# Two rearrangements in a four-layer transformer kernel: the first token half's output part moved into the last attention turn, the second half's beside the last layer; block transposes of the first attention done four groups at a time

## The reference, cut to what matters

```python
x = x + _layernorm(_L0_attn_ref(_layernorm(x)))  # delta-rule attention in chunks of 32 tokens
x = x + _layernorm(_L0_ffn_ref(_layernorm(x)))   # 4-head attention and a mixture of 8 experts
x = x + _layernorm(_L1_attn_ref(_layernorm(x)))  # 16-head attention, then the output part below
x = x + _layernorm(_L1_ffn_ref(_layernorm(x)))   # the last layer: w1, w2, h1, h2, w3
```

```python
A = where(strict_lower, -einsum('bhnck,bhnjk->bhncj', k_beta, k), 0)
for i in range(1, 32): A[..., i, :] += einsum('bhnj,bhnjc->bhnc', A[..., i, :], A)
T = A + eye(32)
local_short, local_long = fir(v, firs), fir(v, firl)
```

```python
out = res + _lin(out, Wf, bf)                                  # wf
return out + _lin(relu(_lin(_ln(out, g2, b2), Wr1, br1)), Wr2, br2)   # hid, ffn
h = silu(tlin(x, w1)) * tlin(x, w2)                            # w1, w2
h = gelu(tlin(gelu(tlin(h, h1)), h2)); return tlin(h, w3)      # h1, h2, w3
```

## Time and profile before

| | us |
|---|---|
| median of 3 runs | 965.95 |
| lowest, highest | 960.08, 970.67 |
| the profiled execution | 958.38 |
| its span, first to last instruction | 956.6 |
| PE, DVE, ACT, POOL busy | 701.7, 583.4, 441.9, 85.3 |
| mean granted clock of TensorE | 0.815 |

### The profile page before, as it was taken

How to read it: one execution, slowest core, us unless ns; L and a number is a source line. 1 busy time by engine, 2 the same in 40 slices (tenths; PEclk the granted TensorE clock), 3 DMA queues, 4 the chain that set the end, 5 groups by cost and what they waited for, 6 DMA issues and landing times. The chain is left out here.

```text
span 956.6 us, 14446 instructions
## 1 busy us (share of the span) xinstructions
PE 701.7 (73%) x5339; PEld 574.5 (60%) x5339; DVE 583.4 (61%) x1332; ACT 441.9 (46%) x907; POOL 85.3 (9%) x98
## 2 busy tenths in 40 slices
PE   3993886998863379550896066999999955659996
PEld 2442786998433248450785043888888844438775
DVE  4118999986286346431332955599998765664474
ACT  3332624543452555320353554555555523467584
POOL 0003202200000100106143002000000001000000
PEclk9997757778885579855698557999999986879998
DMA  5200090000600100002111023111111000000000
GB/s 165 45 0 0 2 152 2 1 1 4 256 1 0 67 1 2 0 3 77 37 32 58 12 88 125 46 45 46 47 55 35 1 1 0 1 1 0 1 23 23
DMA packets 36675, 34.85 MB, mean 36 GB/s; under 512 B 18448, under 2 KB 34704, under 8 KB 35840
## 3 DMA queue, kind: packets, MB, share of 16 engines
q1 hardware_dynamic: 35360, 31.38, 11.1%
q0 software_dynamic: 1248, 2.57, 0.8%
HBM read 20.32 MB, written 5.23 MB: 27 GB/s over the span
## 5 line engine op out<-in xcount | busy, mean ns | idle before, releaser
L2271 PE MATMUL PS<-VXF,PT 128*128 128x128 f32 x1024 | 129.8, 280 | 2.1 <-ACT PT L2293 2.1
L2271 PEld LDWEIGHTS PS<-VXF,PT 128*128 128x128 f32 x1024 | 119.5, 192 | 9.6 <-ACT PT L2293 2.9
L2379 DVE TENSOR_REDUCE MX<-PS 128x2 f32<-128x512 f32 x128 | 81.8, 687 | 30.5 <-PE PS L2236 30.3
L2293 ACT ACTIVATE PT<-PS 128x512 f32<-128x512 f32 x128 | 68.6, 596 | 19.5 <-PE PS L2241 19.4
L2308 ACT ACTIVATE UB<-PS 128x292 f32<-128x292 f32 x64 | 26.5, 415 | 60.2 <-PE PS L2271 60.2
L404 PE MATMUL PS<-XT,WT 128*128 x96 | 42.3, 595 | 1.0 <-ACT XT L290 1.0
L2233 PE MATMUL PS<-SPLIT 32*128 32x256 f32 x256 | 39.3, 325 | 3.1 <-DVE MX L2379 3.1
L1908 ACT ACTIVATE HT<-PS,PB 128x128 f32<-128x128 f32 x92 | 26.3, 368 | 24.4 <-PE PS L1866 18.7
L2606 ACT ACTIVATE PB<-PS,PB 128x512 f32<-128x512 f32 x48 | 33.0, 698 | 7.7 <-PE PS L2521 7.7
L2723 DVE TENSOR_TENSOR HBL<-PB,HBH 128x512 fp32r<-128x512 f32 x32 | 22.1, 690 | 22.6 <-ACT PB L2606 17.5
L2236 PE MATMUL PS<-SPLIT 32*128 32x256 f32 x256 | 32.4, 334 | 3.6 <-DVE MX L2379 2.4
(11 more groups left out here) (471 smaller groups left out, 1759.2 us busy)
## 6 DMA issues: line engine op xcount, KB each, us to landing
SPLIT<-SPLIT SPq DMA_DIRECT2D x64, 128.0 KB, 2.1
PB<-in_pb SPq DMA_DIRECT2D x1, 5016.0 KB, 17.9
PB<-in_pd SPq DMA_DIRECT2D x1, 2888.0 KB, 10.1
X<-in_x SPq DMA_DIRECT2D x2, 1024.0 KB, 4.8
X<-fir_rows SPq DMA_DIRECT2D x2, 1024.0 KB, 6.6
TR<-fir_rows SPq DMA_DIRECT2D x2, 1024.0 KB, 8.6
PA<-in_pa SPq DMA_DIRECT2D x1, 1731.0 KB, 8.5
PC<-in_pc SPq DMA_DIRECT2D x1, 1560.0 KB, 6.4
```

The costliest lines, as they stand in the source:

```text
L2271: last = nc.tensor.matmul(PS[:, UM.bank(n), col:col + P], PT[:, k % 4, c, f * P:(f + 1) * P], v, start=(c == 0), stop=(c == 1))
L2293: nc.scalar.activation(PT[:, k % 4, :, :], PS[:, UM.bank(n), :].rearrange("p (c q) -> p c q", c=2), ACT.Exp).then_inc(c_act, 1)
L2379: nc.vector.tensor_reduce(MX[:, :, k], PS[:, UP_.bank(n), :].rearrange("p (f q) -> p f q", f=2), AX.X, ALU.max, negate=True).then_inc(p_dv ...
```

## The change

First attention. (1) The windows and fir 0 and 1 come first on PE, and DVE empties fir 0 and 1. (2) The short filter stands ahead of invert(0). (3) ACT gathers the four diagonal blocks into `BLOCKS`, DVE transposes all 128 partitions by one instruction, the same at the end of the inversion, and ACT spreads the result into `TBD`, for x = 0 after fir 6, for x = 1 after `"ws"` of half 0.

```diff
+            for w in range(2):
+                events += [(("win", w, j), "A", next_bank()) for j in range(4)]
+            events += [(("fir", e), "V", [8 - EARLY + e]) for e in range(EARLY)]
...
-                        pe.wait_ge(a2_tbd, 4 * x + 4)
+                        pe.wait_ge(a2_spread, 4 * x + 4)
...
+                            if (q, h) == (1, NH - 1):
+                                F.wait_taken(act, key)
+                                if x:
+                                    act.wait_ge(a2_in, x)
+                                for c in range(4):
+                                    own = slice(SUB * c, SUB * c + SUB)
+                                    copy(BLOCKS[own, :, :], GR[x][own, :, own]).then_inc(a2_read, 1)
...
+                        if key in (("fir", 6), ("ws", 0)):
+                            x = int(key[0] == "ws")
+                            act.wait_ge(a2_tbd, x + 1)
+                            for c in range(4):
+                                own = slice(SUB * c, SUB * c + SUB)
+                                copy(TBD[own, :, own], TURNED[own, :, :]).then_inc(a2_spread, 1)
...
-                        for c in range(4):
-                            own = slice(SUB * c, SUB * c + SUB)
-                            nc.vector.transpose(S[own, :, :], GR[x][own, :, own].rearrange("p u j -> p j u"))\
-                                .then_inc(a2_read, 1)
+                        nc.vector.transpose(S, BLOCKS[:, :, :].rearrange("p u j -> p j u")).then_inc(a2_in, 1)
...
-                            nc.vector.transpose(TBD[own, :, own].rearrange("p u i -> p i u"),
-                                                S[own, :, :].rearrange("p j i -> p i j")).then_inc(a2_tbd, 1)
+                        nc.vector.transpose(TURNED.rearrange("p u i -> p i u"), S.rearrange("p j i -> p i j"))\
+                            .then_inc(a2_tbd, 1)
```

```diff
+            events = [(("cols", 0), "V", [2]), (("ot", 0), "A", [0, 1]), (("br", 0), "V", [3]), (("wf", 0), "V", [2, 3]),
+                      (("nt", 0), "A", [0, 1])]
...
+                    if g == 0 and (kind, s_) == ("w2", 0):
+                        events += [(("wf", 1), "V", [6, 7])]
+                    if g == 0 and (kind, s_) == ("h1", 0):
+                        events += [(("nt", 1), "A", [4, 5])]
+                    if g == 0 and (kind, s_) == ("h1", 1):
+                        events += [(("hid", 1, n, c), "A", [(6, 7, 4, 5)[2 * n + c]]) for n in range(2) for c in range(2)]
+                        events += [(("ffn", 1, n), "V", [6 + n]) for n in range(2)]
...
+                if g == 0:
+                    events += [(("xt", 2 + n), "V", [4 + n]) for n in range(2)]
...
+                    pool.wait_ge(e_laid, 1)
+                    for x in range(2):
+                        nc.gpsimd.tensor_tensor(halves(XL, x), halves(XL, x), rows(pc("bf"), 8), ALU.add)\
+                            .then_inc(e_shift, 1)
...
+                    take_all("h2", 0, 1)
+                    finish_norm(4)
+                    normed(4)
+                    V.link(add_norm(halves, 1))
+                    ask_root(5)
+                    finish_norm(5)
+                    take(("w3", 0, 0))
+                    take(("w3", 0, 1))
+                    take(("xt", 2))
+                    take(("xt", 3))
```

More of the change, by code:

```diff
@@ L596, in grams, with fir @@
                                     last.then_inc(a2_full, 1)
-                    for x in range(2):
-                        for kind in ("k", "kb"):
-                            for q in range(2):
-                                turn(kind, x, q)
-                        for q in range(2):
-                            F.wait_taken(pe, ("k", x, q))
-                            F.wait_taken(pe, ("kb", x, q))
-                            grams("low", x, q, KBT, KTR, HALF * x)
-                        for q in range(2):
-                            turn("q", x, q)
[L609 to L617, removed]
+                    def fir(e):
                         F.wait_empty(pe, ("fir", e))
@@ L763, in _ @@
                     copy = lambda dst, src: nc.scalar.activation(dst, src, ACT.Copy)
+                    for w in range(2):
+                        for j in range(4):
+                            take(act, copy, ("win", w, j), a2_act)
                     a_sqrt(NT * NH)
@@ new lines, in _ @@
+                    UM.open(act, "A")
+                    every_batch(scores, project_next, nothing, nothing, weighted, nothing, finish_early, during_last)
+                    take(("hid", 0, 0, 0))
+                    take(("hid", 0, 0, 1))
+                    finish_early(("end", 0), B - 1)
+                    take(("hid", 0, 1, 0))
+                    take(("hid", 0, 1, 1))
+                    for n in (1, 2):
+                        take_root(n)
+                        apply(n)
+                    take(("xt", 0))
@@ new lines, in _ @@
+                    take(("xt", 1))
+                    take(("ot", 1))
+                    take_all("w1", 0, 0)
+                    take_all("w1", 0, 1)
+                    take_root(3)
+                    for n in range(4):
+                        high_gated(0, 1, n)
+                    apply(3)
+                    take_all("h1", 0, 0)
+                    take(("nt", 1))
+                    take_all("h1", 0, 1)
+                    for n in range(2):
+                        for c in range(2):
+                            take(("hid", 1, n, c))
@@ L2320, in _ @@
+                    for n in range(4):
+                        high_gated(1, 1, n)
+                    for kind, s_ in (("h1", 0), ("h1", 1), ("h2", 0), ("h2", 1)):
+                        take_all(kind, 1, s_)
+                    for n in (8, 9):
+                        take_root(n)
+                        apply(n)
                 @block.vector
@@ L2724, in _, with take_all @@
                                     .then_inc(e_split, 1)
[L2725 to L2733 removed]
+                    def take_all(kind, g, s_):
+                        for c in range(4):
+                            take((kind, g, s_, c))
@@ new lines, in _ @@
+                    finish_step(("start", 0), B - 1)
+                    finish_step(("end", 0), B - 1)
+                    finish_step(("weigh", 0), B - 1)
+                    take(("ffn", 0, 0))
+                    take(("ffn", 0, 1))
+                    ask_root(1)
+                    finish_step(("weigh", 1), B - 1)
+                    finish_norm(1)
+                    normed(1)
+                    V.link(add_norm(halves, 0))
+                    ask_root(2)
+                    finish_step(("sum", 0), B - 1)
@@ L2734, in _ @@
+                    take_all("w2", 1, 1)
+                    for n in (6, 7):
+                        normed(n)
+                        add_norm(quarter, n - 6).then_inc(e_final, 1)
+                    for kind, s_ in (("h1", 0), ("h1", 1), ("h2", 0), ("h2", 1)):
+                        take_all(kind, 1, s_)
+                    take(("w3", 1, 0))
+                    take(("w3", 1, 1))
                     for n in (8, 9):
```

584 lines of the change are left out of this document (308 added, 276 removed).

## The result

| | before | changed |
|---|---|---|
| median, first comparison (4 executions each) | 968.24 us | 937.85 us |
| ratio, 95% interval | | 0.9694 [0.962, 0.9768] |
| median, second comparison (11 and 6) | 964.35 us | 934.76 us |
| ratio, 95% interval | | 0.9705 [0.9649, 0.9761] |
| spans of the profiled executions | 956.6 us | 936.3 and 927.4 us |

The changed kernel is 3% faster. I have two profiles of it, here called *first* (936.3) and *second* (927.4). They are the same program, so what differs between them is no effect of an edit.

A forecast was written before the change was run, and what follows sets the result against it. It saw small DVE-ACT-PE pieces bounding attention's end to `w1`, then PE, and DVE's inversions in the first attention. Terms -1 + 2 + 6.2 - 40.0 + 9.4 + 8.6 = -14.8 from 963.8 gave 949.0 us, range 934 to 961.

The forecast's parts named there:

- first attention and all up to POOL's casts: First attention with single transposes and new filter order: -1 us, between -4 and +5.
- POOL's additions: `bf` additions moved from DVE to POOL, meeting DVE's small copies behind the first maxima: +2 us, from 0 to +2.7.
- last turn: Half 0's added PE work and ACT's table loads in the last turn: +6.2 us; 4.6 without ACT waiting, 11 in series.
- attention's end to w1: Stretch from the attention's last matmuls to `w1` of group 0: 26.0 us in place of 66.0, so -40.0.
- w1 to the end of h2, group 0: Inside group 0, half 1's nt, hid and ffn added on PE, +1.0 from DVE: +9.4 us; below, 7.4.
- to h1 of group 1: Behind group 0, half 1's last two norms and w3 statistics precede `xt`: 26.5 against 17.9, +8.6 us.
- rest: From h1 of group 1 on, nothing changes.
- The tail's terms: Terms from POOL's additions to h1 of group 1: +2, +6.2, -40.0, +9.4 and +8.6 us.
- The wait for ACT: In the last turn, two table loads and a root, 2.8 us in one place, make PE wait 1.4 us.
- `ll` at 141.2 + 10.7 = 151.9: First attention, half 0: spread, fir 7, squarings and `fs` copies counted serially behind the inversion; `ll` 2.5 us before 154.44.
- The base of 963.8: Mean of the four known executions of the kernel before, from which the -14.8 us were taken to give 949.0.
- The skill's price for the switches: Last turn: 1.28 us load plus 1.38 drain per switch; two new switches would add 2.8 us, forecast 951.7.

The follow-up runs named there:

- half0_behind: Changed kernel with half 0's cols, ot, br, wf, root 0 and nt run behind the last turn instead of inside it; 948.43 us, ratio 0.9861.
- attn_only: Kernel before with only the edits of the first attention, third layer and last block as before; ratio 0.9887 against before.
- tail_only: Kernel before with all edits except the first attention's, so third layer and last block as changed; 946.0 us, ratio 0.98.
- four_turns: Changed kernel with four 32-partition transposes in and four out per inversion again, without ACT's gathering and spreading, new filter order kept; 947.71 us, ratio 0.9835.
- bf_later: Changed kernel with POOL's two bias additions waiting until DVE has copied the first turned maxima; 932.26 us, ratio 0.9686.
- late_stats: Changed kernel with w3 0 and 1 statistics behind xt 2 and 3 on DVE, their roots behind group 1's w1 on ACT; 935.47 us, ratio 0.9717.
- half1_ahead: Changed kernel with half 1's wf, nt, hid, ffn and norms moved ahead of group 0, in front of xt 0 and 1; 953.34 us.
- second_switch: Changed kernel with one more 8-column root on ACT in step 2 of the last turn, so another pair of table loads; 935.72 us, one execution.
- squares_first: Changed kernel with ACT taking fir 7 and the two squarings before it waits for the first inversion; 931.52 us, ratio 0.9704.

## Why the prediction was right, and where it was not

| step | predicted | first profile | second |
|---|---|---|---|
| first attention and all up to POOL's casts | -1 | -4.9 | -10.5 |
| POOL's additions | +2 | +1.6 | +1.3 |
| last turn | +6.2 | +6.8 | +5.2 |
| attention's end to w1 | -40.0 | -41.4 | -41.4 |
| w1 to the end of h2, group 0 | +9.4 | +9.4 | +8.3 |
| to h1 of group 1 | +8.6 | +9.0 | +8.7 |
| rest | 0 | -0.8 | -0.8 |
| sum | -14.8 | -20.3 | -29.2 |

**What held.** The tail's terms add up to -13.8 as predicted, -15.4 and -18.7 as read. Each came in within 1.5 us. Two printed sums are off by a little: the terms of the last turn (5.0 - 0.4 + 1.4) give 6.0 and not 6.2, and those from the attention's end to `w1` give 25.8 and not 26.0 (measured: 24.66). The path to `w1` was built of the rows of single operations, and half0_behind gave back the 17 us that the same rows make of half 0's chain. That the two halves of the change don't meet was assumed; attn_only and tail_only show it.

**The last turn** has two values, 26.4 and 28.0, in the executions of several kernels. The windows of its end, first and second profile:

```profile
773.00:780.30 7.30, 7.30 (x54) 6.83 (x54) 0.00 (x0) 3.54 (x7) 2.24 (x1) 0.80 0.01 2
```

```profile
767.20:773.00 5.80, 5.80 (x53) 5.40 (x52) 0.00 (x0) 3.51 (x8) 2.24 (x1) 1.00 0.00 0
```

The same matmuls took 1.5 us longer at a clock of 0.80. The wait for ACT was sized right (1.38, in both profiles, for 1.4), the work of PE was not: without the clock's share the turn grew by 5.2, so 3.9 of it are PE's added work, where 4.6 was forecast. In the first profile the clock's 1.5 us, which no term had, lie on top, and 6.8 stands against 6.2: part of that nearness is luck, since the two errors go opposite ways.

**What failed: the first attention.** Two steps. First, in "`ll` at 141.2 + 10.7 = 151.9" I let `ll`'s first bank be `fs`'s third. The `fs` banks are 2 to 5, and `ll` takes 0 to 7 in order, so two tiles go out right behind the spread, while ACT squares. By the rows 1.43 us of PE's waiting were left of what I had counted as serial. Second, the size: I set the shift of `ll` of half 1 near that of half 0, less a loss for the clock, and gave -1 with +5 to -4. The first `y` copy came 7.0 us earlier in the first profile (6.7 in the second), and `ll` of half 1 6.2 and 12.0. Of the 6 us between the 0.75 us expected at the end of `ll` and the 7.0 measured, 0.9 are the inversion (out of DVE at 140.3, not 141.2) and the rest is `ll` beside ACT's squarings in place of behind them. The transposes themselves were sized right (1.9 against 2.0), and taking them back in four_turns moved the first `y` by 7.0 us (9.2 by the clock of the profile, of which 2.1 are there at the first scaling).

**From profile to median.** Forecast 949.0, measured 937.85, 11 us apart. The miss in what the change does is larger: 14.8 us forecast, and 30.4 and 29.6 measured in the medians of the two comparisons. The base of 963.8 lay 4.4 below the median of the kernel before in the first comparison (968.24; 964.35, 964.05 and 965.89 in the others), and that hid a part of it. The profiled execution, 958.38, lay low among them; from that one I would have been at 943.6, nearer, with the same sum and for no better reason.

More traces than the two profiles of the changed kernel have the same first attention, so its term can be read again. From the first scaling of q to POOL's casts, the eight traces with the new first attention and without the squarings' edit (bf_later, late_stats, half0_behind, half1_ahead and second_switch among them) have 475.3 to 484.8 us, 479.1 in the mean; the two with the old one have 485.95 and 492.87, 489.4 in the mean. That is -10.3, as attn_only's ratio says (-10.9, interval -5 to -17), where the forecast had -1; 7.7 of it are there at `ll` of half 1 (92.0 to 98.5 against 102.8 and 104.0). From the casts to the end, the five traces with the whole new tail (first, second, tail_only, four_turns, squares_first) have 359.9 us in the mean, against 376.6 and 377.1: -16.9, where the forecast had -13.8 (tail_only's ratio: -19.3). So some 9 us of the miss are the first attention and some 3 the tail.

**The skill's price for the switches.** By the price in the Trainium skill (ScalarE: Activation LUTs, What ACT_TABLE_LOAD costs) the two drains would have added 2.8 us in the turn, an estimate (2 x 1.38). In all loads shown above the next instruction starts 1.29 to 1.30 us behind the load's own start, and a further pair cost 0.2 us of turn. The rows decide against the added drain.

## What to carry over

Block-diagonal 32x32 blocks that sit in four partition groups are worth gathering by an idle engine, so that one 128-partition transpose does the work of four: here ACT had 8 us free and DVE saved 13 us for each half. When a chain moves off a critical stretch, write the bank numbers of the old and new users beside each other before adding up what is serial. And when a queue's next instruction feeds another engine (`xt` for `w1`), move statistics and roots that nobody waits for behind it, and a norm whose input is ready into a stretch where its engine has a half microsecond free in each piece.

## What was not expected of the hardware

One program differs from itself in one stage by more than some edits bring. Windows of half 0's states and outputs, first and second profile:

```profile
170.00:180.00 10.00, 9.20 (x151) 9.02 (x149) 10.00 (x5) 5.13 (x13) 1.88 (x3) 0.74 0.01 2
180.00:191.81 11.81, 11.12 (x74) 10.83 (x74) 2.37 (x2) 6.44 (x6) 0.00 (x0) 0.73 0.00 0
```

```profile
170.00:180.00 10.00, 9.22 (x167) 9.05 (x165) 10.00 (x5) 4.77 (x12) 1.53 (x2) 1.00 0.01 2
180.00:186.09 6.09, 5.40 (x49) 5.21 (x48) 2.65 (x2) 5.03 (x6) 0.00 (x0) 1.00 0.00 0
```

`ll` started within 0.3 us of each other (144.67, 144.93), and `ll` of half 1 at 191.81 and 186.09. The windows do not hold the same work, since the first was some 3 us behind by then; the same matmuls are these, first and second profile, from the first `ws` to the last outputs:

```profile
181.74 0.50 PE L722 MATMUL PS<-Y,PA 128*128 128x128 f32 x2
190.25 1.75 PE L709 MATMUL PS<-Y,PB 128*128 128x32 f32 x8
```

```profile
178.89 0.47 PE L722 MATMUL PS<-Y,PA 128*128 128x128 f32 x2
185.28 0.98 PE L709 MATMUL PS<-Y,PB 128*128 128x32 f32 x8
```

From the first `ws` to `ll` of half 1 they took 10.07 and 7.20 us, at a granted clock of 0.68 and 1.00 over just these stretches; the `y` steps before them took 26.51 and 23.39 at 0.68 and 0.78. From `ll` of half 0 to `ll` of half 1 there are 47.1 and 41.2 us, and squares_first had 36.8. The Trainium skill (TensorE: Matmul & The Clock Gate, Part 1: The HAM clock gate) says that the ramp varies between runs of a kernel, and puts its penalty below 1% of a typical span. The first agrees. As to the second, this one stage moved by 5.9 us, 0.6% of the span; the six executions of the changed kernel lie 9.3 us apart (929.17 to 938.47), and how much of that is the clock no run shows. Edits of 1 to 2 us could be read only from the stretches of the trace that touch them, never from the totals.

What stays open: where the last 2.6 of the 10.3 us of the first attention come from. Between `ll` of half 1 and POOL's casts all kernels of this study took 379.4 to 390.0 us with the same instructions, and the only two traces with the old first attention lie at 382.0 and 390.0. attn_only's profiled execution (957.33) was the slowest of its six and that of the kernel before (958.38) among its quickest, which is why their spans differ by only 1.0 us where the medians differ by about 10.
